# An adaLN block with attention and experts: the first batch's projection order, root statistics and six split positions changed

## The reference

```python
sa, ca, ga, sb, cb, gb = silu(c) @ wmod             # six blocks of 256 per batch
h = layernorm(x) * (1 + ca) + sa
q, k, v = h @ wq, h @ wk, h @ wv                    # 16, 4 and 4 heads of 128
q = q * cos + rotate_half(q) * sin                  # k the same
q = q / (norm(q, per head) + 1e-6) * query_scale    # k the same, with key_scale
scores = tanh(q @ k.T / sqrt(128) / 50) * 50
scores = where(abs(i - j) <= 128, scores, -inf)
x = x + ga * ((softmax(scores) @ v) @ wo)
h2 = layernorm(x) * (1 + cb) + sb
x = x + gb * sum_e w_e * ((silu(h2 @ Wg[e]) * (h2 @ Wu[e])) @ Wd[e])
```

## Time and profile before

| | |
|---|---|
| time, median of 3 runs | 820.75 us (820.59 to 824.83) |
| the profiled execution's own time | 819.02 us |
| its span | 817.3 us |
| PE, DVE, ACT, POOL busy | 98%, 67%, 51%, 48% |
| mean granted PE clock | 0.998 |
| bytes moved | 21.50 MB, mean 26 GB/s |

### The profile page before, as it was taken

How to read it: one execution, slowest core, us unless ns; L and a number is a source line. 1 busy time by engine, 2 the same in 40 slices (tenths; PEclk the granted TensorE clock), 3 DMA queues, 4 the chain that set the end, 5 groups by cost and what they waited for, 6 DMA issues and landing times.

```text
span 817.3 us, 14284 instructions
## 1 busy us (share of the span) xinstructions
PE 798.9 (98%) x5116; PEld 710.9 (87%) x5116; DVE 551.5 (67%) x1154; ACT 418.9 (51%) x694; POOL 395.4 (48%) x543
## 2 busy tenths in 40 slices
PE   8889999999999999999999998999999999999997
PEld 7667999999999998898998997998888888888886
DVE  5688776567668668668669758866785555454575
ACT  3665666566656656656656655652352232332322
POOL 2696677567567567567657556220010110110492
PEclk9999999999999999999999999999999999999999
DMA  8200010000000000000000000202210110100002
GB/s 327 103 28 2 14 47 1 1 8 1 1 5 5 1 2 7 1 2 8 1 1 8 2 2 1 78 1 45 85 39 1 39 40 1 38 1 1 2 1 103
DMA packets 8021, 21.50 MB, mean 26 GB/s; under 512 B 1544, under 2 KB 4232, under 8 KB 7824
## 3 DMA queue, kind: packets, MB, share of 16 engines
q1 hardware_dynamic: 7376, 20.51, 7.5%
q10 hardware_dynamic: 576, 0.08, 0.1%
HBM read 18.48 MB, written 2.11 MB: 25 GB/s over the span
## 4 chain that ended last, share of the span: by engine, by line
PE 90%; DVE 6%; issue 2%; POOL 1%; DMA 1%; ACT 0%; SPq 0%; DVEq 0%; POOLq 0%; ACTq 0%
PE ps_o L593 13%; PE ps_proj L487 9%; PE ps_proj L489 9%; PE ps_proj L488 9%; PE ps_s L487 7%; PE ps_s L488 7%; PE ps_s L489 7%; PE ps_turn L537 4%; PE ps_y L487 3%; PE ps_y L488 3%; PE ps_y L489 3%; PE ps_turn L546 3%; PE ps_turn L487 2%; PE ps_turn L488 2%; PE ps_turn L489 2%; DVE prod L1073 2%
## 5 line engine op out<-in xcount | busy, mean ns | idle before, releaser
L593 PE MATMUL ps_o<-vaug,probs 128*128 128x129 f32 x1024 | 135.4, 275 | 4.5 <-DVE o_rows L1107 2.9
L593 PEld LDWEIGHTS ps_o<-vaug,probs 128*128 128x128 f32 x1024 | 128.8, 191 | 11.6 <-issue 4.4
L873 ACT ACTIVATE ps_s<-ps_s,knorm 128x512 f32<-128x512 f32 x128 | 79.2, 657 | 107.5 <-PE ps_s L489 107.5
L1421 POOL TENSOR_TENSOR root<-ssq,powers 128x4 f32<-128x4 f32 x80 | 82.8, 1034 | 86.1 <-DVE ssq L1070 86.0
L1457 POOL TENSOR_TENSOR we_lo<-raw_e,we_hi 128x512 fp32r<-128x512 f32 x22 | 28.4, 1315 | 184.1 <-ACT we_hi L916 184.1
L1103 DVE RECIPROCAL rden<-ps_o 128x2 f32<-128x2 f32 x128 | 21.6, 169 | 130.9 <-PE ps_o L593 130.6
L1073 DVE TENSOR_TENSOR prod<-ps_proj,cs 128x1024 f32<-128x1024 f32 x80 | 97.1, 1214 | 0.0
L487 PE MATMUL ps_proj<-w_hi,h_hi 128*128 128x512 f32 x192 | 83.3, 434 | 0.5 <-DVE prod L1073 0.3
L1437 POOL TENSOR_TENSOR prod<-prod 128x512 f32<-128x512 f32 x64 | 82.4, 1287 | 0.0
L487 PE MATMUL ps_y<-wo_hi,oT_hi 128*128 128x256 f32 x256 | 75.8, 296 | 0.0
L489 PE MATMUL ps_proj<-w_hi,h_lo 128*128 128x512 f32 x192 | 75.7, 394 | 0.0
(11 more groups left out here) (184 smaller groups left out, 2179.4 us busy)
## 6 DMA issues: line engine op xcount, KB each, us to landing
raw_e<-in_we SPq DMA_DIRECT2D x8, 768.0 KB, 4.3
raw_p<-in_wqkv SPq DMA_DIRECT2D x6, 512.0 KB, 9.1
raw_e<-in_wo SPq DMA_DIRECT2D x4, 512.0 KB, 12.8
x_all<-in_x SPq DMA_DIRECT2D x1, 1792.0 KB, 7.7
out<-acc SPq DMA_DIRECT2D x3, 512.0 KB, 2.6
x_all<-in_wmod SPq DMA_DIRECT2D x1, 1024.0 KB, 10.8
gates_a<-gate_rows_dram SPq DMA_DIRECT2D x8, 128.0 KB, 2.9
gates_b<-gate_rows_dram SPq DMA_DIRECT2D x1, 1024.0 KB, 8.2
```

The lines of the kernel that those rows point to most:

```text
L593: mm = pe.matmul(ps_o[:, h * (D + 1):(h + 1) * (D + 1)], probs[:, s % 2, at:at + P], vaug[b % 2][:, k, i // 2, :], start=(h == 0 and k == ...
L873: act.activation(ps_s[:, t, :], ps_s[:, t, :], ACT.Tanh, scale=knorm[:, b % 2, t, i // 2:i // 2 + 1]).then_inc(tanh_done, 1)
L1421: pool.tensor_tensor(root[:, n % 2, :], ssq[:, n % 2, :], powers[:, 0:4], ALU.pow).then_inc(root_ready, 1)
```

## The change

For batch 0 a list of its own, `PROJ_FIRST`, puts both value units behind the first two query units; `unit(b, p)` picks the list. Of what follows, the prediction speaks:

```diff
+PROJ_FIRST = [("k", 0, 0), ("k", 0, 1), ("q", 0, 0), ("q", 0, 1), ("v", 0, 0), ("v", 0, 1),
+              ("q", 1, 0), ("q", 1, 1), ("q", 2, 0), ("q", 2, 1), ("q", 3, 0), ("q", 3, 1)]
+NORMS = 4
-FIRST_TURN = {-2: (0, 1), -1: (2, 3), 0: (4,), 1: (5,), 2: (6, 7), 3: (8, 9)}
+FIRST_TURN = {-2: (0, 1), -1: (2, 3), 1: (4, 5), 2: (6, 7), 3: (8, 9)}
+FIRST_NORM = [2, 3, 0, 1]
-SLOT_SPLIT = {-3: [2], -2: [3], -1: [4], 0: [5], 1: [6], 3: [7], 5: [8], 7: [9]}
+SLOT_SPLIT = {-3: [2], -2: [3], -1: [4], 1: [5], 2: [6], 3: [7], 5: [8], 7: [9]}
-SLOT_H2 = {56: [0], 57: [1], 59: [2, 4], 60: [3, 5], 63: [6]}
-SLOT_EXPERT = {57: [(0, 0)], 58: [(0, 1)], 60: [(0, 2)], 62: [(1, 0), (1, 1)], 63: [(1, 2)]}
+SLOT_H2 = {52: [0], 53: [1], 55: [2], 56: [3], 59: [4], 60: [5], 63: [6]}
+H2_AFTER = [2, 4, 7, 8]
+SLOT_EXPERT = {57: [(0, 0), (0, 1)], 60: [(0, 2)], 62: [(1, 0), (1, 1)], 63: [(1, 2)]}
...
 PE, at the start:
-            keep_busy(12)
+            keep_busy(8)
+            pe.wait_ge(zeros_rounded, 1)
+            for n in [P] * 12 + [P // 2] * 12:
+                pe.matmul(ps_s[:, 1, 0:n], h_hi[:, 0, 0:P], h_hi[:, 0, 0:n], ...)
 PE, project, for the two key units of batch 0:
+                        if (b2, unit(b2, p2)[0]) == (0, "k"):
+                            pe.wait_ge(square_ready, rot_of(b2, p2) + 1)
 ACT, ahead of the Silu:
+            act.wait_ge(zeroed, 1)
+            act.activation(h_hi[:, 0, 0:P], probs[:, 0, 0:P], ACT.Copy).then_inc(zeros_rounded, 1)
 ACT, square, for the same two units:
+                    if (b, unit(b, p)[0]) == (0, "k"):
+                        act.wait_ge(rotated, n + 1)
 DVE, rotate: the sum of squares is now total(b, p); the key units of batch 0 leave it out there
+                if (b, unit(b, p)[0]) == (0, "k"):
+                    dve.wait_ge(proj_ready, p + 1)
+                else:
+                    total(b, p)
 DVE, slot:
+                if s == 1:
+                    norm_stats(1)
+                if s == FIRST:
+                    for p in range(TT):
+                        total(0, p)
-                if i == 0 and 0 <= b < B - 1:
+                if i == 0 and 0 < b < B - 1:
                     norm_stats(b + 1)
+                if s == FIRST + 2:
+                    for p in range(TT):
+                        inverse(0, p)
 POOL, slot:
-                if i == 1 and 0 <= b < B - 1:
+                if i == 1 and 0 < b < B - 1:
                     inv_std(b + 1)
+                if s == FIRST + 2:
+                    for p in range(TT):
+                        norm_of(0, p)
                 for bb, p in units[:1]:
-                    norm_of(bb, p)
+                    if s > FIRST:
+                        norm_of(bb, p)
                     unit_rows(bb, p)
+                if s == 1:
+                    inv_std(1)
```

More of the change, by code:

```diff
@@ L94, with unit, rot_of, norm_at @@
 SHARED = 60
-def rot_of(p):
-    return ROT.index(PROJ[p])
+def unit(b, p):
+    return PROJ[p] if b else PROJ_FIRST[p]
+def rot_of(b, p):
+    return ROT.index(unit(b, p))
+def norm_at(n):
+    return FIRST_NORM.index(n) if n < len(FIRST_NORM) else n
 def live(s):
@@ L118, in turns_of, with ahead @@
     return first + [(b + later, r) for later, r in SLOT_TURN[i] if 0 < b + later < B]
+def ahead(s):
+    return 2 if s == 1 else 1
 def turns_h(s):
@@ L225, in build @@
         shift2 = sb("shift2", [P, NT])
-        ssq = sb("ssq", [P, 2, 4])
-        root = sb("root", [P, 2, 4])
-        roote = sb("roote", [P, 2, 4])
-        rnorm = sb("rnorm", [P, 2, 4])
+        ssq = sb("ssq", [P, NORMS, 4])
+        root = sb("root", [P, NORMS, 4])
+        roote = sb("roote", [P, NORMS, 4])
+        rnorm = sb("rnorm", [P, NORMS, 4])
         knorm = sb("knorm", [P, 2, TT, 4])
@@ L549, in project @@
             def project(b, p):
-                kind, g, t = PROJ[p]
+                kind, g, t = unit(b, p)
                 u = NP * b + p
@@ L707, in slot @@
                     weighted(s - 1, 1)
-                for bb, r in turns[:1]:
+                for bb, r in turns[:ahead(s)]:
                     turn_rows(bb, r)
@@ L711, in slot @@
                     project(bb, p)
-                for bb, r in turns[1:]:
+                for bb, r in turns[ahead(s):]:
                     turn_rows(bb, r)
@@ L732, in _ @@
             pe.wait_ge(zeroed, 1)
-            keep_busy(12)
+            keep_busy(8)
+            pe.wait_ge(zeros_rounded, 1)
+            for n in [P] * 12 + [P // 2] * 12:
+                pe.matmul(ps_s[:, 1, 0:n], h_hi[:, 0, 0:P], h_hi[:, 0, 0:n], start=True, stop=True, skip_group_check=True)
             pe.wait_ge(silu_c, 1)
@@ L825, in square @@
                 act.wait_ge(proj_ready, u + 1)
-                if PROJ[p][0] == "v":
-                    t = PROJ[p][2]
+                if unit(b, p)[0] == "v":
+                    t = unit(b, p)[2]
                     if b >= 2:
@@ L996, in _ @@
             split_w(1)
+            split_w(2)
             slot(FIRST)
@@ L1306, in slot @@
                     rotate(bb, p)
-                for bb, r in turns[:1]:
-                    turned_tail(bb, r)
+                for bb, r in turns[:ahead(s)]:
+                    if s > FIRST + 1:
+                        turned_tail(bb, r)
                 for bb, p in units[:1]:
-                    inverse(bb, p)
+                    if s > FIRST:
+                        inverse(bb, p)
                 for bb, p in units[1:]:
                     rotate(bb, p)
-                for bb, r in turns[1:]:
+                if s == FIRST:
+                    for p in range(TT):
+                        total(0, p)
+                if s == FIRST + 1:
+                    for bb, r in turns[:1]:
+                        turned_tail(bb, r)
+                for bb, r in turns[ahead(s):]:
                     turned_tail(bb, r)
-                if i == 0 and 0 <= b < B - 1:
+                if i == 0 and 0 < b < B - 1:
                     norm_stats(b + 1)
@@ L1414, in norm_of @@
             def norm_of(b, p):
-                if PROJ[p][0] == "v":
+                if unit(b, p)[0] == "v":
                     return
-                n = NR * b + rot_of(p)
+                n = NR * b + rot_of(b, p)
                 pool.wait_ge(summed, n + 1)
-                if n >= 2:
-                    pool.wait_ge(rnorm_ready, n - 1)
-                pool.tensor_tensor(root[:, n % 2, :], ssq[:, n % 2, :], powers[:, 0:4], ALU.pow).then_inc(root_ready, 1)
-                pool.wait_ge(root_ready, n + 1)
-                pool.tensor_tensor(roote[:, n % 2, :], root[:, n % 2, :], powers[:, 12:16], ALU.add).then_inc(eps_added, 1)
+                if n >= NORMS:
+                    was, r = divmod(n - NORMS, NR)
+                    if ROT[r][0] == "k":
+                        pool.wait_ge(knorm_ready, TT * was + r + 1)
+                    else:
+                        pool.wait_ge(rnorm_ready, NQ * was + r - TT + 1)
+                pool.tensor_tensor(root[:, n % NORMS, :], ssq[:, n % NORMS, :], powers[:, 0:4], ALU.pow).then_inc(root_ready, 1)
+                pool.wait_ge(root_ready, norm_at(n) + 1)
+                pool.tensor_tensor(roote[:, n % NORMS, :], root[:, n % NORMS, :], powers[:, 12:16], ALU.add).then_inc(eps_added, 1)
             def unit_rows(b, p):
-                if PROJ[p][0] == "v":
+                if unit(b, p)[0] == "v":
                     return
-                n = NR * b + rot_of(p)
+                n = NR * b + rot_of(b, p)
                 turned = prod[:, n % 2, 1].rearrange("p h (a d) -> p h a d", a=2)[:, :, ::-1, :]
@@ L1431, in unit_rows @@
                 pool.wait_ge(rotated, n + 1)
-                if PROJ[p][0] == "k":
+                if unit(b, p)[0] == "k":
                     if n >= RING:
```

57 lines of the change are left out of this document (32 added, 25 removed).

## The result

The changed kernel takes 830.82 us (median of 4 runs, 830.75 to 832.87) against 820.67 us (4 runs, 819.87 to 824.83) of the kernel before on the same chip: a ratio of 1.0121, 95% interval 1.0092 to 1.0150. It is 10.1 us slower. The forecast was 827.0 us, with a range of 822.5 to 831.0. The profiled execution took 830.75 us, with a span of 829.0 and a mean granted clock of 0.989. The ratios are of the fast runs alone (one run of the kernel with both blocks back, 1161.27 us at a granted clock of 0.645, is left out of its ratio), and they differ from the quotients of the two medians by up to 0.0012.

The account below looks back on a forecast made before the run. PE, busy for 98% of the span, was taken to bound the kernel. The terms +7.1 -0.2 -1.35 +0.8 summed to +6.35 us, giving 827.0 us from 820.75, with a range of 822.5 to 831.0.

Parts of the forecast that it names:

- Block 5: Ahead of q30's projection: late `inv_std(1)` on POOL delays block 5; PE stands 4.7 us and is 2.5 us late.
- Block 6: Ahead of the first output projection: block 6's split behind `h_lo` makes PE start at 64.0 instead of 56.91, 7.1 us later.
- The start: Before the first projection: rounded zeros fill PE's idle stretch and may keep its clock up, -0.2 us (0 to -0.3).
- The head start: At first scores: the new order lets scores(0) start at about 30.2 instead of 33.00, 2.8 us sooner.
- scores(0) starts at 30 to 30.5: Sign that the forecast is right: first scores on PE start at 30 to 30.5 us.
- a clock of 1.00 from 8 to 12 us: Sign that the forecast is right: PE's granted clock stays at 1.00 from 8 to 12 us, at the start.
- The clock in the stalls: Behind PE's two new stalls: a possible fall of the clock, set at +0.8 us, bounds none and 3.2.
- Rival 1: Clock falls in both stalls, 1.6 us lost each: +8.75 us, 829.5 us; chance 0.18.
- The late part: Slots 52 to 57: the 1.49 us `we_lo` gap goes, the 0.89 us gap grows by about 0.15; -1.35 us.
- Nothing is given back between 60 and 80 us: After the first output projection: the DVE chain behind the 70 to 80 us gaps starts equally later, so the delay stays.
- Rival 4: Loss partly given back between 60 and 80 us, as most of 1.6 us of gaps go: 825.4 us; chance 0.12.
- rivals 2 and 3: 2: POOL early enough, only block 6 stalls, 821.6 us, chance 0.14. 3: block 6 early too, 817.0 us, chance 0.08.

Follow-up runs that it names:

- the kernel with both blocks back: Changed kernel with blocks 5 and 6 split in slots 0 and 1 again, as before the change: 823.75 us against 821.08, ratio 1.0029.
- the filled kernel: Changed kernel with 17 and 20 unused products on PE just ahead of its two long waits: 827.17 us, ratio 1.0083 to the kernel before.
- the kernel with the start back: Changed kernel with `keep_busy(12)` and without the rounded zeros: 827.54 us, ratio 1.0083 to the kernel before.

## Why the prediction was right, and which terms were mis-sized

- **Block 5 (+2.5 us at q30, +5.3 from scores(0)).** Right, in place, releaser and size: +5.38. POOL's units took the 3.6 us that the earlier trace rows gave, and `inv_std(1)` 1.5. What the prediction didn't see is that the wait covered a second lateness: slot 2's tanh "in time for scores(3)" was in time only because PE stood. With block 5 in slot -1 it shows as waits of 2.15 and 1.20 us.
- **Block 6 (+4.6 us from the transpose).** Right: +5.22. The copy and `h_lo` came in the order forecast; the split took 2.19 us, above the middle that was chosen, since it began 0.15 us after POOL's addition at 65.65 and ended 1.1 us after the addition did (66.91). By "SBUF — State Buffer" of the Trainium skill, whoever comes first holds the shared ports: the trace agrees, 2.19 us here against 1.19 alone.
- **The start (-0.2).** Wrong in sign. The step that failed is "if the clock stays up". It did not stay up: it was low for 6.9 us, where it had been low for 3.4 before (the prediction took 3.2). By ratios the start costs 0.0024 to 0.0038, 2 to 3 us, in the three pairs of kernels that differ in it. That little was to be won there was right: a clock of 1.00 throughout brought the first projection at 11.65 to 11.88 in three executions and at 12.60 in a fourth, against 12.43 before.
- **The head start (-2.8).** Right in mechanism and, with the old start, in size: scores(0) at 29.69 and 30.01, against 32.25 to 33.00 in kernels with the old order and start. In the changed kernel the start took it back, 0.71 us was left: against the kernel with the start back, the first projection came 1.68 us later and its twelve products took 0.93 us more at the low clock, together 2.6 us, the whole way from 29.69 to 32.29. The sign "scores(0) starts at 30 to 30.5" failed with it, as did the one of a clock of 1.00 from 8 to 12 us.
- **The clock in the stalls (+0.8, bounds 0 and 3.2).** Mis-sized: 3.8 us by rows, 3.1 by the ratio of the filled kernel. Rival 1's mechanism happened, and its 829.5 us was nearer to the measured time than the forecast. Its price of 1.6 us for each stall was not: they cost 1.34 and 2.49. The middle was chosen from the 1.86 us gap, which is less than half as long as the stalls; the row nearest in kind was the emptiest one, at the start.
- **The late part (-1.35).** Right: -1.74 by rows, -2.8 (-4.4 to -1.2) alone.
- **Nothing is given back between 60 and 80 us.** Right: the lag of 13.7 us at weighted(2) is still 13.4 us at the gap near 500 us. Rival 4 fell, and with the POOL times and the order on DVE rivals 2 and 3.

The forecast's sum was +6.35 us, the profiled pair differs by 11.7: 2.3 of the difference are the first stretch, 3.0 the clock, 0.7 the two stalls, less 0.7 in the late part. Between the medians it is +10.1 us, which is 0.2 us inside the range: that the time fell in it is luck as much as judgment, since the mis-sized start and clock had used up nearly all of it. The sum's own upper end was +10.1, and the profiled pair lies above that.

## What to carry to other kernels

A stall that a trace shows is priced by what is late behind it: ask what else waits for the same releaser (here the tanh queued behind the rows that waited for `inv_std(1)`), or its removal gives little (block 5 back in slot 0: 1 us or less by ratio, where 3.0 us of wait and a low clock behind it stood). A wait of several us on PE costs its length and then the clock, which in these runs added 1.3 and 2.5 us to 4.3 and 5.0. When the order on one engine is changed, list what every other engine has queued between its old and its new place: here one small `inv_std` behind a 3.6 us unit on POOL stood at the head of what made slot 2 late. And look at what a moved instruction runs beside: a split on DVE, started just ahead of a step on POOL, cost POOL 1.0 us.
